# Layer 9's preparation issued in another order, with parts of its softplus on VectorE and GpSimd

## The reference

```python
def _L3_attn_ref(x, in_proj_w, conv_w, conv_b, x_proj_w, dt_proj_w, dt_proj_b, out_proj_w, A_log, D_param):
    proj = x @ in_proj_w
    hidden, gate = jnp.split(proj, 2, axis=-1)
    h = jnp.swapaxes(hidden, 1, 2)
    h = jax.lax.conv_general_dilated(h, conv_w, window_strides=(1,), padding=((KCONV - 1, KCONV - 1),), feature_group_count=INTER)[..., :L]
    h = h + conv_b[None, :, None]
    hs = jnp.swapaxes(jax.nn.silu(h), 1, 2)
    ssm_p = hs @ x_proj_w
    dt, Bm, Cm = jnp.split(ssm_p, [DTRANK, DTRANK + NSTATE], axis=-1)
    Bm, Cm, dt = (_rms(Bm), _rms(Cm), _rms(dt))
    dt = jax.nn.softplus(dt @ dt_proj_w + dt_proj_b)
    A = -jnp.exp(A_log)
    dA = jnp.exp(dt[..., None] * A)
    dBu = (dt * u)[..., None] * Bm[:, :, None, :]      # u is hs
    # over the tokens t:  s = dA_t * s + dBu_t;  y_t = sum over the states of s * C_t
    y = (y + u * D_param) * jax.nn.silu(gate)
    return y @ out_proj_w
```

## Time and profile before

| | |
|---|---|
| median of 3 runs | 1835.78 us (1832.43 to 1838.63) |
| the profiled execution | 1814.33 us |
| its span, first to last instruction | 1812.5 us |
| TensorE busy | 1642.5 us, 91% |
| VectorE busy | 1163.1 us, 64% |
| ScalarE busy | 927.9 us, 51% |
| GpSimd busy | 685.9 us, 38% |
| mean granted TensorE clock | 0.947 of full speed |

### The profile page before, as it was taken

How to read it: one execution, slowest core, us unless ns; L and a number is a source line. 1 busy time by engine, 2 the same in 40 slices (tenths; PEclk the granted TensorE clock), 3 DMA queues, 4 the chain that set the end, 5 groups by cost and what they waited for, 6 DMA issues and landing times. The chain is left out here.

```text
span 1812.5 us, 29616 instructions
## 1 busy us (share of the span) xinstructions
PE 1642.5 (91%) x9892; PEld 1214.2 (67%) x9908; DVE 1163.1 (64%) x3187; ACT 927.9 (51%) x2344; POOL 685.9 (38%) x870
## 2 busy tenths in 40 slices
PE   7998999899999988876999788888799898999997
PEld 6886677778888864444888636665577554555786
DVE  4455667557777774654555454786455557999867
ACT  3212788445555556752343205653344279999342
POOL 1113312223333241333333324547333225999412
PEclk9999989899999998986999999879999999999999
DMA  6002610266390006014343430001533501111021
GB/s 246 30 30 66 125 33 2 99 218 214 130 318 9 1 1 279 25 37 147 117 127 95 169 142 24 1 16 70 161 104 102 203 21 48 52 47 47 1 71 47
DMA packets 52537, 166.52 MB, mean 92 GB/s; under 512 B 8474, under 2 KB 29722, under 8 KB 48003
## 3 DMA queue, kind: packets, MB, share of 16 engines
q1 hardware_dynamic: 39570, 131.80, 21.5%
q0 software_dynamic: 10080, 24.69, 4.2%
q10 hardware_dynamic: 2736, 8.13, 1.5%
HBM read 135.62 MB, written 64.79 MB: 111 GB/s over the span
## 5 line engine op out<-in xcount | busy, mean ns | idle before, releaser
L201 PE MATMUL ps<-R 128*128 128x512 f32 (+4 forms) x1824 | 320.8, 342 | 18.4 <-ACT AR L1601 9.7
L204 ACT ACTIVATE AR<-AR 128x128 f32<-128x128 f32 (+3 forms) x547 | 266.5, 556 | 128.1 <-DVE AR L218 94.0
L201 PEld LDWEIGHTS ps<-R 128*128 128x128 f32 (+1 forms) x1824 | 256.6, 194 | 68.7 <-ACT AR L1601 12.9
L326 PEld LDWEIGHTS ps<-cf,AR 128*128 128x128 f32 (+1 forms) x1134 | 139.9, 143 | 127.4 <-issue 59.5
L201 PE MATMUL ps<-AR 64*128 64x128 f32 (+6 forms) x1374 | 213.9, 330 | 8.9 <-DVE AR L207 4.8
L326 PE MATMUL ps<-cf,AR 128*128 128x128 f32 (+1 forms) x1134 | 199.0, 285 | 19.2 <-DVE AR L207 6.8
L201 PE MATMUL ps<-W,AR 128*128 128x256 f32 (+3 forms) x1184 | 197.8, 343 | 7.9 <-ACT AR L1619 7.9
L201 PEld LDWEIGHTS ps<-AR 128*128 128x128 f32 (+2 forms) x1374 | 157.3, 189 | 38.9 <-issue 25.6
L201 PEld LDWEIGHTS ps<-W,AR 128*128 128x128 f32 (+2 forms) x1184 | 150.0, 160 | 36.3 <-issue 17.4
L207 POOL TENSOR_TENSOR AR<-AR,CR 128x512 f32<-128x512 f32 x128 | 162.7, 1277 | 12.1 <-DVE AR L221 10.3
L221 DVE TENSOR_TENSOR_SCAN AR<-AR,ps 128x512 f32<-128x512 f32 x128 | 155.4, 1219 | 17.6 <-PE ps L326 8.6
(11 more groups left out here) (283 smaller groups left out, 3059.5 us busy)
## 6 DMA issues: line engine op xcount, KB each, us to landing
xs<-in_zero SPq DMA_DIRECT2D x33, 1060.0 KB, 32.5
Y<-xs SPq DMA_DIRECT2D x110, 132.5 KB, 2.1
W<-in_wts SPq DMA_DIRECT2D x4, 2048.0 KB, 8.1
CR<-shd SPq DMA_DIRECT2D x32, 256.0 KB, 3.1
W<-in_wts SPq DMA_DIRECT2D x5, 1280.0 KB, 7.5
WL<-in_gl SPq DMA_DIRECT2D x3, 2048.0 KB, 12.3
AR<-in_gs SPq DMA_DIRECT2D x1, 6144.0 KB, 31.4
W<-zs SPq DMA_DIRECT2D x12, 512.0 KB, 6.7
```

Of the source, the lines that this page charges most:

```text
L201: return self.e.matmul(o, l, r, start=start, stop=stop, skip_group_check=True)
L204: return self.e.activation(o, i, f, bias=bias, scale=scale)
L326: return e.e.transpose(o, i, ident[0:n, 0:n])
```

## The change

The same functions of the input are computed. The tiles of four temporaries move to a weight slot that is free at that time, and so the second of the two chunks of layer 11's weights (1920 KB) is loaded later: at the start of the scan, no longer at the end of layer 8. The orders on all four engines are rewritten; the second half's Relu goes to VectorE (`dve_relu`), and the subtraction of max(v, 0) from the correction goes to GpSimd (`pool_merge`), so that `dve_fed` has two passes in place of three. The core of the diff:

```diff
-                self.temps = [... for a in (turned[:, 0:2048], turned[:, 2048:4096], decays[:, 0:2048], H) for k in range(2)]
+                self.temps = [... for a in (turned[:, 0:2048], turned[:, 2048:4096], W[:, 0, 0:2048], W[:, 0, 2048:4096]) for k in range(2)]
...
             def sum_bank(self, n, c):
-                return banks[6 + c] if n and c < 2 else banks[c]
+                return banks[(c, (6, 7, 0, 1)[c])[n]]
...
             def pe_direct(self, e, n, c):
-                e.mm(self.sum_bank(n, c), self.D[:, c, :], self.u[n][:, c, :], True, False)
+                e.mm(self.sum_bank(n, c), self.D[:, c, :], self.u[n][:, c, :], self.opens(n, c), False)
...
                 if n and nn == 0 and c >= 2:
-                    e.wait_ge(*T.gatedout.at(c + 1))
-                    self.pe_direct(e, n, c)
+                    e.wait_ge(*T.gatedout.at(c - 1))
...
                 for i in range(130):
-                    if i + 1 < 128:
+                    if i and i + 1 < 128:
                         self.pe_inflow(e, i + 1)
+                    if i < 2:
+                        for c in range(2):
+                            e.wait_ge(*T.ducopied.at(5 + 2 * i + c))
+                            self.pe_direct(e, 1 - i, 2 * i + c)
+                    if i >= 128:
+                        self.pe_direct(e, 1, i - 126)
                     if i >= 2:
                         self.pe_sum(e, i - 2)
...
+            def dve_relu(self, e, m, k):
+                e.wait_ge(*self.T.absexp.at(m + 1))
+                e.ts(self.d[m // 4][:, m % 4, :], k, smc("db")[:, m % 4:m % 4 + 1], ALU.add, 0.0, ALU.max)
+            def pool_merge(self, e, m):
+                e.wait_ge(*T.onemore.at(m + 1))
+                e.tt(x[:, 0, :], x[:, 0, :], self.d[m // 4][:, m % 4, :], ALU.subtract).then_inc(T.merged.sem, 1)
             def dve_fed(self, e, m):
+                e.wait_ge(*T.merged.at(m + 1))
                 e.wait_ge(*T.logged.at(m + 1))
-                e.tt(x[:, 1, :], x[:, 1, :], x[:, 0, :], ALU.subtract).then_inc(e.sem, e.up())
-                e.settle()
-                e.tt(self.d[n][:, c, :], x[:, 1, :], self.d[n][:, c, :], ALU.add).then_inc(e.sem, e.up())
+                e.tt(self.d[n][:, c, :], x[:, 1, :], x[:, 0, :], ALU.subtract).then_inc(e.sem, e.up())
                 e.settle()
                 e.wait_ge(*T.silued.at(m + 1))
                 e.tt(x[:, 1, :], self.d[n][:, c, :], self.u[n][:, c, :], ALU.mult).then_inc(T.fed.sem, 1)
...
                 for c in range(4):
-                    self.dve_fed(e, c)
-                for c in range(4, 8):
-                    self.dve_one_more(e, c)
-                for c in range(4, 8):
-                    self.dve_fed(e, c)
+                    self.dve_relu(e, 4 + c, late[c])
+                    self.dve_one_more(e, 4 + c)
+                for m in range(8):
+                    self.dve_fed(e, m)
...
-                    if 64 <= i < 68:
-                        self.dve_gated_out(e, 0, i - 64)
+                    if i in (64, 66, 74, 82):
+                        self.dve_gated_out(e, 0, (64, 66, 74, 82).index(i))
...
             def act_absexp(self, e, m, k):
-                e.act(self.d[m // 4][:, m % 4, :], k, ACT.Relu, bias=db)
+                if m < 4:
+                    e.act(self.d[0][:, m, :], k, ACT.Relu, bias=db)
...
                 e.wait_ge(*N[8].added.at(8))
-                for k in range(first_chunk[11], len(sizes)):
-                    weights(k)
+                weights(first_chunk[11])
...
+                e.wait_ge(*layers[9].T.duturned.at(8))
+                weights(first_chunk[11] + 1)
                 for q in range(3, 32):
                     layers[9].sp_spread_C(e, q)
```

More of the change, by code:

```diff
@@ L4122, in __init__ @@
                 self.temps = [quarters(a)[:, 2 * k:2 * k + 2, :] for a in (turned[:, 0:2048], turned[:, 2048:4096],
-                                                                            decays[:, 0:2048], H) for k in range(2)]
+                                                                            W[:, 0, 0:2048], W[:, 0, 2048:4096]) for k in range(2)]
                 self.taps = quarters(g0[:, 0:512])
@@ L4151, in pe_xproj, with pe_conv @@
                 t.then_inc(T.xproj.sem, 1)
[L4153 removed]
+            def pe_conv(self, e, n, k, begin=0, end=4):
                 T, h3 = self.T, self.HP[(4 * n + 3) % 3]
@@ L4156, in pe_conv @@
                 e.wait_ge(*T.filled.at(4 * n + 4))
-                for i in range(4):
+                for i in range(begin, end):
                     t = e.mm(k.rearrange("p (b t) -> p b t", b=4), self.taps[:, i, :], h3[:, :, i:i + 128], i == 0, i == 3)
-                t.then_inc(T.summed4.sem, 1)
+                if end == 4:
+                    t.then_inc(T.summed4.sem, 1)
             def pe_in(self, e, q, k):
@@ L4243, in pe @@
                 T, eight = self.T, layers[8]
+                near = banks[0], banks[1], banks[4], banks[5]
+                late = banks[3], banks[6], banks[7], banks[2]
+                far = banks[6], banks[7], banks[2], banks[3]
                 e.wait_ge(s_rot, 16 * 9)
@@ L4269, in pe @@
+                self.pe_dproj(e, 1, near[1])
+                for b in range(4, 7):
+                    self.pe_xproj(e, b, late[b - 4])
+                self.pe_dproj(e, 2, near[2])
+                self.pe_xproj(e, 7, late[3])
+                self.pe_dproj(e, 3, near[3])
                 for c in range(4):
-                    self.pe_dproj(e, c, banks[2 + c])
-                late = banks[6], banks[0], banks[1], banks[7]
+                    e.wait_ge(*T.absexp.at(c + 1))
+                    self.pe_gate(e, 4 + c, near[c])
@@ L4272, in pe @@
                 for b in range(4, 8):
[L4273 to L4279 removed]
+                    self.pe_turn_parts(e, b, late[b - 4])
                 for c in range(4):
@@ L4367, in dve @@
                 T, l = self.T, self.l
+                late = banks[3], banks[6], banks[7], banks[2]
                 layers[8].dve_sum(e, 4)
                 self.dve_conv(e, 0)
-                for b in range(5, 8):
-                    layers[8].dve_sum(e, b)
-                    dve_norm(e, 8, b - 1)
+                layers[8].dve_sum(e, 5)
+                dve_norm(e, 8, 4)
+                self.dve_conv(e, 1, 0, 2)
+                layers[8].dve_sum(e, 6)
+                dve_norm(e, 8, 5)
+                layers[8].dve_sum(e, 7)
+                dve_norm(e, 8, 6)
                 dve_norm(e, 8, 7)
-                self.dve_conv(e, 1)
-                for q in (2, 4, 5, 6):
+                self.dve_conv(e, 1, 2, 4)
+                for q in (2, 4, 5):
                     self.dve_conv(e, q)
@@ L4499, in act @@
                 self.act_silu(e, 0)
+                act_copy_state(e, 8, 4)
+                act_copy_state(e, 8, 5)
                 self.act_fill(e, 3, banks[6])
-                for b in range(4, 8):
-                    act_copy_state(e, 8, b)
+                act_copy_state(e, 8, 6)
+                act_copy_state(e, 8, 7)
                 self.act_silu(e, 1)
@@ L4577, in pool @@
                 e.wait_ge(*T.summed4.at(2))
+                for m in range(4):
+                    self.pool_merge(e, m)
                 for c in range(4):
@@ L4584, in pool @@
                 t.then_inc(T.cleared.sem, 1)
+                for m in range(4, 8):
+                    self.pool_merge(e, m)
                 for i in range(128):
```

147 lines of the change are left out of this document (74 added, 73 removed).

## The result

Twenty executions of each kernel gave 1823.28 us (1809.80 to 1832.19) for the changed one and 1832.29 us (1814.93 to 1841.61) for the one before; the ratio is 0.9953, 95% interval 0.9933 to 0.9974. The forecast was 1831.2 and a range down to 1827.3, so the result lies outside it. The median of before had been 1835.78 with three runs, and is 3.5 us lower with twenty.

What follows compares the result with a forecast made beforehand. TensorE bounds the scan loop, ScalarE mostly the preparation ahead; in the new order VectorE sets the first decay. Terms -3.7 - 2.4 + 1.45 = -4.6 give 1809.7 profiled, 1831.2 carried to the median; whole range 1827.3 to 1835.3.

Steps and rivals of the forecast that it cites:

- first Exp table: ScalarE's first Exp table load in layer 8's preparation: at 1465.7 in place of 1468.30, 2.6 us earlier.
- last Exp: End of ScalarE's last exponential in the preparation: at 1487.4 in place of 1495.26, 7.8 us earlier in all.
- hold by the merges: In the preparation, GpSimd's last four merges block VectorE: three times 0.72 and once 1.00, 3.16 us.
- first decay: ScalarE's first decay, before which the scan loop cannot start: at 1504.3 in place of 1509.76, 5.5 us earlier.
- 11th scan: Start of TensorE's steady scan loop, forecast at 1521.1; 3.7 us won there, 0.4 of it from the clock.
- middle: 65th to 72nd scan: moving two directs to the end and spreading the gated products wins 2.4 us.
- tail: End of the scan loop: two directs now precede the last two sums, costing 1.45 us.
- stretch: From the last group of layer 8's gathers on TensorE to the output projection; forecast sum 4.6 us shorter.
- Rival A: Merges hold VectorE not or only in part, so ScalarE bounds the preparation: -6.8 us, 1829.0; chance 0.17.
- Rival C: Each ScalarE table switch also idles for as long as its load: -7.1 us, 1828.7; chance 0.06.
- Rival D: Waits of 2.6 us in the ramp that laying the order end to end misses: -2.0 us, 1833.8; chance 0.09.
- Rival B: TensorE's low clock after short turns reaches into the ramp and loop: +0.7 us, 1836.5; chance 0.08.

Runs made afterwards that it cites:

- the split logarithms: Changed kernel with the first half's four logarithms back between the halves' exponentials, so six table loads; ratio 0.9985 to the kernel before.
- the late weights: Kernel before with only the second chunk of layer 11's weights loaded at the start of the scan; ratio 1.0015 to the kernel before.

## Why the prediction was wrong

Measured from the gather, in the two first profiles:

| step | forecast | measured |
|---|---|---|
| first Exp table | -2.6 | -2.64 |
| last Exp | -7.8 | -7.87 |
| hold by the merges | 3.16 | 2.85 |
| first decay | -5.5 | -5.58 |
| 11th scan | -3.7 | -4.19 |
| middle | -2.4 | -2.31 |
| tail | +1.45 | +1.31 |
| stretch | -4.6 | -5.20 |

**The terms were right.** The order laid end to end gave every point to about 0.1 us up to the first decay, the hold came as the rows of other layers had it, and the experiments that undid one term each moved the decay or the scans by what the sum had: tables and loop to 0.15 us, the merges to 0.3 (1.94 for 2.2). Rival A, no hold, is refuted by 1.06 for 0.42. The rule of the Trainium skill ("SBUF — State Buffer", § "Who interferes with whom"), that the later of the two blocks for the whole instruction, agrees: the pass that began 0.49 into a merge of 1.27 ended 0.28 behind it. Rival C, a dearer switch, is refuted by the split logarithms, 3.3 and not 5.8. The 2.66 us of "ScalarE: Activation LUTs" in the Trainium skill (§ "What ACT_TABLE_LOAD costs") is not what these traces show: the first decay starts 1.30 behind its table load (1515.20 and 1516.50 above). The transfer is hidden. Rival D's waits weren't there.

**The step that failed** is the last one of the sum, "the median of the runs, 1835.78, is 1.2% above the profile, and I carry the difference over". The result is 7.9 us under the forecast, and this step has two faults. The first is the base, the median of three runs, 3.5 us above that of twenty. The second is the gain, 9.0 us between the medians for the 4.6 of the sum: the profiled execution of before was taken for all of them. It was the one of four without a lowered clock behind the turns, so what the change removes there, 0 in the row, is 1.4 and 1.6 us at the first Exp table with 3.4 us of it and 2.8 with 6.8, about 1.5 on average. I looked for the clock only where a row showed it, ahead of the loop, and in rival B only for a loss. The four waits in a row are a pattern like the one that had the lowered clock in the earlier trace rows, where the turns of the fed tiles stand with waits of 1.33, 1.43, 1.33 and 0.97 ahead of them:

```profile
1499.53 0.63 PE L326 MATMUL ps<-cf,AR 128*128 128x128 f32 x4 [1.33 <-DVE AR L207]
1501.59 0.72 PE L326 MATMUL ps<-cf,AR 128*128 128x128 f32 x4 [1.43 <-DVE AR L207]
1503.64 1.09 PE L326 MATMUL ps<-cf,AR 128*128 128x128 f32 x4 [1.33 <-DVE AR L207]
1505.69 1.09 PE L326 MATMUL ps<-cf,AR 128*128 128x128 f32 x4 [0.97 <-DVE AR L207]
```

I priced the first four by their 2.62 us of idle time and not by what may follow. Of the 4.4 us that the sum lacks, the average stretches show 1.4, these 1.5 less small terms. Another 1.2 is the rest of the program, not clear of its scatter, and 1.8 stay open; the interval of the ratio reaches from 4.8 to 12.3 us.

The ramp in the two first profiles was 0.5 more than forecast. The new order's own count, the 11th scan at 1521.1 or 83.11 behind the gather, was right within 0.2 (82.92); 0.3 was lost by mixing in the old order's count, 1524.3 where its trace has 1525.1. (3.2 and 0.4 are also 3.6 and not 3.7, and two decays, 1.9 and ten of 0.617 are 9.3 where the text adds 9.0.) It was also luck that the changed kernel's first profile had no lowered clock there, which cost 0.8 and 1.1 us in its two others; on average the ramp is no part of the miss.

And the range was too narrow for a base of three runs. From 1832.29 the same sum gives 1827.7, and 1823.28 is still 4.4 below; the whole range would be 1823.8 to 1831.8, and the result 0.5 outside it.

**Rival B**, the clock as a loss, had its mechanism right (short turns with waits lower it) and its price wrong: it cost the changed kernel 0.8 and 1.1 us for 6.8 of it, and the old order had its own in all four profiles.

## What to carry to other kernels

Several short waits of TensorE in a row can cost more than their idle time (here a lowered clock followed 18 of 20 such lulls that were left open): look at the granted clock behind them, in more than one profile, and put independent matmuls between the dependent ones. Whether an operation moved to GpSimd is free depends on what VectorE does beside it: the passes with two inputs in SBUF, and those with one and constants, were held for 0.64 to 0.96 us by an operation of 1.27, the Relu from PSUM not at all, so move only what falls where VectorE is ahead. A sum from one profiled execution is good to 0.1 us for what the orders fix, and blind for what happens in some executions only.

## What was not expected of the hardware

The same program has the lowered clock at a place in one execution and not in another: the kernel before had none, 3.4, 3.4 (with the late weights) and 6.8 us of it behind its turns. It costs about half of its time where TensorE is the bound (1.4 and 1.6 us for 3.4, 2.8 for 6.8), and less at the start of the loop, where ScalarE is: 0.8 and 1.1 for 6.8, nothing for 3.4. With matmuls that nothing reads in TensorE's waits it was absent in all five profiles at the fed tiles, where 10 of 11 have it otherwise; the one profile at the turns had none either, which by itself shows little. The program's median also differs between the sets by up to 19 us (1813.02 to 1832.29 for the kernel before; on two known chips 1813.02 and 1828.36), so only times of one set were compared.
